# Forty mixing steps beside the first batch's last three attention iterations, dealt out anew as 15, 15 and 10

## What is computed

```python
# layer 0, for every token: four streams of 128 channels
H_res = (1.0 - g) * I + g * sinkhorn_log(H_res_logits)      # 4 x 4 per token
x_mixed = jnp.einsum('btij,btjc->btic', H_res, x_streams)
y_distributed = jnp.einsum('btc,btn->btnc', y, H_post)
out = x_mixed + y_distributed
...
# layer 1, for every batch: 32 heads of 128, keys and values shared by 4 heads
scores = jnp.einsum('bhqd,bhkd->bhqk', q, k) * scale
attn = jax.nn.softmax(jnp.where(causal, scores, -1e9), axis=-1)
out = jnp.einsum('bhqk,bhkd->bhqd', attn, v)
out = out.transpose(0, 2, 1, 3).reshape(b, s, H * D) @ Wo.T
```

## Time and profile before

| | |
|---|---|
| median of 3 executions | 2323.69 us (2314.49 to 2326.49) |
| the profiled execution: time | 2323.69 us |
| its span, first to last instruction | 2321.9 us |
| granted TensorE clock over the span | 0.988 of full speed |
| attention of the first batch | about 354 to 1270 us |
| one iteration of it | about 112.4 us |

### The profile page before, as it was taken

One profiled execution on the slowest core, in us unless ns is written; L12 is line 12 of the kernel. 1 busy time (PEld: TensorE's weight loads), 2 busy tenths in 40 slices (PEclk: granted clock), 3 DMA queues, 4 the chain that ended last, 5 costly groups with the idle time before them and its releaser, 6 DMA issues. The chain is left out here.

```text
span 2321.9 us, 34666 instructions
## 1 busy us (share of the span) xinstructions
PE 2221.4 (96%) x11190; PEld 1808.9 (78%) x11190; DVE 1541.8 (66%) x3818; ACT 1069.9 (46%) x2282; POOL 1016.8 (44%) x1124
## 2 busy tenths in 40 slices
PE   6899899999999999999997989999999999999998
PEld 5554687888888888888885777888888888888886
DVE  6778576777677777767575474656666666666565
ACT  2456234545544454545453332545454545444454
POOL 5341814444445353758583012434444443435241
PEclk9999999999999999999999999999999999999999
DMA  9600573010101011011201373010101010101000
GB/s 344 219 1 9 225 275 112 10 63 10 63 24 49 27 46 36 36 53 37 66 7 42 159 286 121 10 64 9 63 9 63 9 63 9 63 17 56 27 33 32
DMA packets 74168, 165.26 MB, mean 71 GB/s; under 512 B 4721, under 2 KB 38897, under 8 KB 67442
## 3 DMA queue, kind: packets, MB, share of 16 engines
q1 hardware_dynamic: 73650, 162.95, 19.9%
q10 hardware_dynamic: 432, 1.32, 0.1%
HBM read 113.40 MB, written 72.61 MB: 80 GB/s over the span
## 5 line engine op out<-in xcount | busy, mean ns | idle before, releaser
L1873 DVE TENSOR_TENSOR pT<-psum,pT 128x512 fp32r<-128x512 f32 x576 | 387.3, 689 | 257.4 <-ACT pT L1921 255.1
L1773 POOL TENSOR_TENSOR probs_even<-probs_even,rinv 128x1024 f32<-128x1024 f32 (+2 forms) x192 | 241.0, 1255 | 537.3 <-DVE rinv L1864 537.3
L1921 ACT ACTIVATE pT<-psum 128x512 fp32r<-128x512 f32 x576 | 331.3, 597 | 311.8 <-PE psum L1982 311.7
L1859 DVE CUSTOM_DVE_ANT_0 psum<-psum,causal 128x256 f32<-128x256 f32 (+7 forms) x512 | 385.9, 767 | 34.3 <-PE psum L98 30.5
L1912 ACT ACTIVATE probs_even<-psum,nmax 128x1024 f32<-128x1024 f32 (+3 forms) x256 | 204.5, 799 | 247.4 <-DVE nmax L1859 244.0
L1773 POOL TENSOR_TENSOR probs_odd<-probs_odd,rinv 128x896 f32<-128x896 f32 (+2 forms) x192 | 198.6, 1042 | 264.1 <-DVE rinv L1864 264.0
L96 PE MATMUL psum<-keys,q 128*128 128x512 f32 (+3 forms) x768 | 265.6, 346 | 3.7 <-DVE q L1814 2.8
L98 PE MATMUL psum<-keys,q 128*128 128x512 f32 (+3 forms) x768 | 262.0, 341 | 0.0
L97 PE MATMUL psum<-keys,q 128*128 128x512 f32 (+3 forms) x768 | 261.9, 341 | 0.0
L96 PE MATMUL psum<-pT,vals 128*128 128x512 f32 x576 | 256.4, 445 | 4.6 <-DVE pT L1873 0.7
L1912 ACT ACTIVATE probs_odd<-psum,nmax 128x896 f32<-128x896 f32 (+3 forms) x256 | 176.6, 690 | 144.0 <-DVE nmax L1859 141.1
(11 more groups left out here) (304 smaller groups left out, 4429.1 us busy)
## 6 DMA issues: line engine op xcount, KB each, us to landing
wq<-wq_copy SPq DMA_DIRECT2D x16, 1024.0 KB, 4.8
k_parts<-kv_out SPq DMA_DIRECT2D x32, 512.0 KB, 3.8
v_parts<-kv_out SPq DMA_DIRECT2D x32, 512.0 KB, 3.7
wo<-wo_copy SPq DMA_DIRECT2D x16, 1024.0 KB, 4.8
keys<-k_parts SPq DMA_DIRECT2D x32, 512.0 KB, 4.7
vals<-v_parts SPq DMA_DIRECT2D x64, 256.0 KB, 3.1
acc<-in_x SPq DMA_DIRECT2D x4, 1024.0 KB, 12.3
xn_later<-xn SPq DMA_DIRECT2D x1, 2048.0 KB, 14.8
```

The lines of the kernel that those rows point to most:

```text
L1773: pool.tensor_tensor(p, p, rinv[:, u, h:h + 1].to_broadcast([P, (TB - u) * P]), ALU.mult).then_inc(p_ok, 1)
L1859: dve.tensor_tensor_reduce(out=row, in0=row, in1=causal[:, S - n:S], scale=-1.0, scalar=-2 * MASKED, op0=ALU.add, op1=ALU.min, accum_out=n ...
L1873: dve.tensor_tensor(pT[:, n % PT_SLOTS, 1, :], bank[T_BANK + n % 2], f32(pT[:, n % PT_SLOTS, 0, :]), ALU.subtract).then_inc(t_lo, 1)
L1921: act.activation(pT[:, n % PT_SLOTS, 0, :], bank[T_BANK + n % 2], ACT.Copy).then_inc(t_hi, 1)
```

## The change

It changes which mixing steps lie in which iteration and behind which norm, and where SP's queue holds the loads for them. The 40 steps and their instructions stay the same.

| iteration | tiles before | steps behind the norms (u: h = 0, 1, 2) before | tiles after | steps after |
|---|---|---|---|---|
| 5 | 0, 1 | 2: 1,1,1; 4: 1,1,1; 5: 1,1,0; 7: 0,0,2 | 0, 1, 2 | 2: 1,1,3; 4: 1,1,2; 5: 1,1,1; 7: 0,0,3 |
| 6 | 2, 3, 4 | 0: 1,1,1; 2: 1,1,1; 4: 1,1,1; 5: 1,1,1; 7: 0,0,3 | 3, 4, 5 | the same as in iteration 5 |
| 7 | 5, 6, 7 | 0: 1,1,1; 2: 1,1,2; 3: 1,1,2; 4: 1,1,2 | 6, 7 | the same table, which runs out after ten steps: 2: 1,1,3; 4: 1,1,2; 5: 1 |

```diff
-            tiles_of = {5: (0, 1), 6: (2, 3, 4), 7: (5, 6, 7)}
-            spread = {0: (1, 1, 1), 2: (1, 1, 1), 4: (1, 1, 1), 5: (1, 1, 1), 7: (0, 0, 3)}
-            mixing_steps = {5: {2: (1, 1, 1), 4: (1, 1, 1), 5: (1, 1, 0), 7: (0, 0, 2)}, 6: spread,
-                            7: {0: (1, 1, 1), 2: (1, 1, 2), 3: (1, 1, 2), 4: (1, 1, 2)}}
+            tiles_of = {5: (0, 1, 2), 6: (3, 4, 5), 7: (6, 7)}
+            mixing_steps = {2: (1, 1, 3), 4: (1, 1, 2), 5: (1, 1, 1), 7: (0, 0, 3)}
...
                 load(wq[:, 1], m.wq_s[g]).then_inc(wq_in, 16)
-                for t in mixed_now[:1]:
+                for t in mixed_now[:2]:
                     later_loads(t + 1)
                 sp.wait_ge(pv_mm, it * TILES + (PV0 + first_tile(4)))
                 for k in range(2):
                     load(vals[:, k, 4:8, :], vals_of(g, k, 1)).then_inc(v_in[1], 16)
-                for t in mixed_now[1:-1]:
+                for t in mixed_now[2:]:
                     later_loads(t + 1)
                 sp.wait_ge(s_mm, it * SC + SC)
                 for k in (1, 0):
                     load(keys[:, k, :], keys_of(g, k)).then_inc(k_in, 16)
...
                 load(wo[:, 1], m.wo_s[g]).then_inc(wo_in, 16)
-                for t in mixed_now[-1:]:
-                    later_loads(t + 1)
...
             if mixes_later:
-                for t in tiles_of[ITERS - 1][:-1]:
-                    later_loads(t + 1)
+                later_loads(TB - 1)
...
-                        if mixes_later and it >= mixing_from and u in mixing_steps[it]:
-                            for _ in range(mixing_steps[it][u][h]):
+                        if mixes_later and it >= mixing_from and u in mixing_steps:
+                            for _ in range(mixing_steps[u][h]):
                                 next(beside, None)
```

## The result

The changed kernel takes 2352.79 us in the median (2350.76 to 2353.61, 4 runs), the kernel before 2325.09 us (2314.49 to 2329.17, 4 runs). The ratio is 1.0125, with a 95% interval of 1.0091 to 1.016: 27.7 us slower. The sign was forecast; the size was forecast at 19.4 us, and the time lies 1.8 us above the range. (The forecast stood on 2323.69 us for the kernel before; with its fourth run the median is 1.4 us higher, which is most of that distance.)

A forecast was written before the change was run, and what follows sets the result against it. PE, busy 96% of the span, was taken as the bound. Terms -5.2 + 3.9 + 2.5 + 1.1 + 8.4 + 7.5 + 1.2 = +19.4 us on 2323.69 gave 2343 us, 0.8% slower; 8-in-10 range 2330 to 2351.

The forecast's parts named there:

- iteration 7 relieved: Iteration 7, turn(4, 0): fewer steps before norm(4, 2) take back PE's wait and the half clock behind it, -5.2 us.
- turn(3, 0), iterations 5 and 6: Two steps more behind norm(2, 2) make PE wait at turn(3, 0): 3.9 us in iteration 5, 2.5 in iteration 6.
- keys, iterations 5 and 6: PE's first scores of the next iteration wait for late keys, 4.2 us in each of iterations 5 and 6, +8.4.
- half clock behind these waits: PE at 1.2 GHz behind the new waits: 7.5 us for the three long ones, 1.2 for the 2.5 us one.
- PE is packed, so waits count in full: PE is busy 96% of the span, so every microsecond it is made to wait is one of the result.
- The room in front of turn(3, 0): Between norm(3, 2)'s end and turn(3, 0): 1.06 us spare in iteration 5, 0.85 in 6, against 4.94 us of added steps.
- The tile boundary in block 5: A tile ends behind norm(5, 0), so the next step awaits a load: +1.1 us in iteration 5, 0 in iteration 6.
- SP's queue holds the keys until the 15th step: The fourth tile's load, in front of the keys, waits for all 15 steps: keys issued 9.8 us later.
- The crowd on the DMA engines: Keys share DMA engines with loads before and behind them: 0.5 us extra wait, from bounds of 0 and 2.4 us.
- The clock: Long PE waits bring half clock, 2.5 us each for three waits plus 1.2 for iteration 6's: 8.7 us.
- the clock holds: Rival: the waits come as computed but PE keeps 2.4 GHz through them, 2334 us; chance 0.16.
- The other side: Rival: iteration 7's relief at turn(4, 0), 5.2 us, outweighs the new steps' cost in iterations 5 and 6, 2318.5 us; chance 0.04.

The follow-up runs named there:

- keys first: The changed kernel with the third tile's load moved behind the load of `wo`, so the keys are issued earlier: 2333.44 us, ratio to the kernel before 1.0023.
- the old table: The kernel before, its table of steps kept, with the last tile's load of iterations 5 and 6 in front of the keys: 2337.18 us, ratio 1.0047.
- the better table: The kernel before, tiles and queue order kept, with other places for the steps of iterations 6 and 7: 2317.9 us, ratio 0.9971.

## Why the prediction was right and wrong

Its own terms, against what stretches between marks of the two profiled executions show (us). Each mark, that is the rows of PE above and their counterparts, is compared after taking off the 1.57 us by which the changed execution was late at the keys of iteration 4; turn(3, 0) of iteration 5, for instance, comes at 995.91 in place of 990.15, which leaves 4.2. The first scores of iteration 7 were at 1155.12 before. What a stretch lost beyond its wait is put down to the clock. In iteration 7 the wait at turn(4, 0) shrinks from 3.80 to 1.37 us, 2.43, and from there to the last addition it was 37.93 us before, 35.45 in the second batch, which has no half clock there, and 37.07 in the changed kernel: the half clock that is gone was worth 2.48, the one that is new in the tail 1.62.

| term | forecast | measured |
|---|---|---|
| iteration 7 relieved | -5.2 | -2.4 - 2.5 = -4.9 |
| turn(3, 0), iterations 5 and 6 | 3.9 + 2.5 | 4.2 + 2.8 |
| turn(5, 0) | 1.1 + 0 | 1.2 + 0.1 |
| keys, iterations 5 and 6 | 4.2 + 4.2 | 6.4 + 5.5 |
| half clock behind these waits | 7.5 + 1.2 | 1.7, 2.4, 1.6 and 2.4, together 8.2 |
| half clock in the tail of iteration 7 | none | 1.6 |
| sum | 19.4 | 25.1 |

- *PE is packed, so waits count in full*: right. Each wait moved everything behind it and none was made up.
- *The room in front of turn(3, 0), by one norm's end against one start, and 2.47 us for a step*: right to 0.3 us, and the step's price is confirmed by taking one away (2.55 and 2.43 us).
- *The tile boundary in block 5*: right, 1.24 us against 1.1. Moving it removes the wait. That POOL would have again its 2.04 us of idle time before norm(4, 0) was too much, since the 1.06 us of room were used up; it has 0.76, still enough.
- *SP's queue holds the keys until the 15th step*: right in place and in lateness (9.84 us), shown from both sides by keys first and by the old table.
- *The crowd on the DMA engines*: this step failed, and the keys' term, 8.4 forecast and 11.9 measured, is the largest miss. The term "I take 0.5, near the lower end", on top of the 3.7 us, measured 6.26 - 3.7 = 2.6 and 5.33 - 3.7 = 1.6 us. I had counted the load in front only by its 0.84 us of issue and read the slow landing of the earlier trace rows as the work of the four loads *behind* those keys. But holding the loads behind back changes nothing, and taking the small load *in front* away shortens the waits by 2.58 and 2.01 us. Those keys too had a load in front of them, `wo`, as the rows above show, and the prediction overlooked it. With 2.1 in place of 0.5 the sum would have been 22.6, the time 2346 us, inside the range.
- *The clock*: right in sum, 8.2 against 8.7, and partly by luck, since the first fall cost 1.7 and not 2.5 us and the wait at turn(3, 0) of iteration 6 could have gone either way. The trace of the kernel before showed that: of its waits of 2.5 to 2.9 us elsewhere, those at 55.65 and 96.43 had half clock, those at 1367.87 and 1397.85 had not. A reading was off: 0.80 and 0.79 in the earlier trace rows put the half clock from 1229.6 to 1236.4, which is 5.2 us of work and a loss of 2.6, not 5.5 and 2.8. The runs show the clock closely. Every one of the 20 waits of 3.3 us or more in iterations 5 to 7 of the kernel before, the changed one and the eight experiments was followed by half clock; of the six waits of 2.8 us at turn(3, 0) of iteration 6 four were; of the 16 waits of 1.6 us or less for POOL at turn(3, 0) and turn(5, 0) none. The same 2.8 us wait shows the price: from turn(3, 0) to turn(5, 0), with the second wait taken off, it is 27.2 us in the changed kernel, where the clock fell, and 25.6 with keys first, where it held, 1.6 us. The Trainium skill (TensorE: Matmul & The Clock Gate, Part 1) states both levels, and that where the switch falls differs from run to run. The waits of 2.8 us agree with it, which have half clock in one run and not in another; those of 3.3 us and more show no such difference, and the rival "the clock holds" found no support.
- *Half clock with no long wait*: not foreseen, a term of 1.6 us that the sum put at nothing. In the changed kernel and four of the experiments the clock also fell in the tail of iteration 7, behind idle times of 1.2 to 1.6 us. It is not the change that does it: in the last iteration of the second batch, where no code differs and the idle times up to there are 1.2 us at most, the clock fell in eight of the ten profiled executions. From the keys' issue in iteration 6 to the last addition these take 121.4 us, and the other two 119.8; the kernel before's, 119.76, is one of the two. Why it falls in some and not in others is open.
- *The other side*: the relief of iteration 7 was worth 4.9 us, nearly as said, and the better table shows it can be had without a price.

The last 2.6 of the 27.7 us, 27.7 - 25.1, are less than what single executions of the same code differ by.

## What to carry to other kernels

Before a wait is put into an in-order DMA queue, look at what stands behind it and how much room that has; a load that nobody is waiting for can cost the one that everybody needs. Side work belongs where the engine has room before the *next* instruction that another engine waits for, and that room is one subtraction between two rows: here 1.06 us, against 4.9 us of added work. Price a late transfer first with what is queued in front of it; here what was queued behind counted for little. And before a difference is put down to a change, compare the stretches whose code is the same.

## What the runs showed of the hardware that was not expected

- 320 KB in two loads issued just in front of 1 MB of keys made these land after 6.9 us in place of 5.3 (first kernel with, second without them), more than the two loads' separate effects together (2.6 against 1.2 + 0.4 us of wait). 1.5 MB issued right behind had no effect there (7.0 with them held back).
- The wait of 2.8 us at turn(3, 0) was followed by half clock in four of six executions, the waits of 3.3 us or more in iterations 5 to 7 in all 20 cases.
- Half clock (1.2 GHz) also came where PE's idle times were 1.2 us at most, in the last iteration of the second batch in eight of ten executions, at a price of 1.6 us (121.4 against 119.8 us).
- Stretches of unchanged code differed by 6.9 us between two single executions, and half clock made 6.4 of it (PE busy 2.85, 1.82 and 1.76 us longer for the same number of products).
